# Slots of destination blocks shared in chains of four instead of pairs

## The chip, the cores and the metric

The kernel runs on one NeuronCore of a Trainium2 chip. The metric is the device time of one execution in microseconds (us), the median of three runs. The trace is that of one further execution, taken by the hardware profiler. A core has five engines that run their own instruction streams side by side: TensorE (PE), VectorE (DVE), ScalarE (ACT), GpSimd (POOL) and SyncE (SP).

## The reference

A graph of 3125 nodes with 128 features and 53125 edges, sorted by destination, passes through four graph layers. After each the result is added to x and normalised:

```python
x = _layernorm(x + _L0_gnn_ref(x, deg_isqrt[:, None], src, dst), axis=-1)   # 10 hops of hs[src] summed by dst
x = _layernorm(x + _L1_gnn_ref(x, edge_index, ...), axis=-1)                # two attention (GAT) layers, 4 heads
x = _layernorm(x + _L2_gnn_ref(x, edge_index, edge_type_8, ...), axis=-1)   # h[edge_type, src] * weight summed by dst
x = _layernorm(x + _L3_gnn_ref(x, src, dst, ...), axis=-1)                  # attention of 8 heads, then an MLP
```

Each of L1 (twice), L2 and L3 reads, for every edge, a row of a table at the edge's source, weighs it, and adds it to the edge's destination (`jax.ops.segment_sum(msg, dst, ...)`). The norms and the dense products between them belong to the nodes, not the edges.

## The kernel before

**Blocks, slots, tiles.** The nodes are cut into 25 destination blocks of 128 (`NB`; the last has 53 nodes). A slot, or tile, is 128 edges, one on each partition. Every one of the first 24 blocks has `CAP = 17` slots and the last has 7 (`CAP_TAIL`), 415 in all. Each node's own loop is taken out of the list and treated by itself, so that a block has some 2050 edges and its 17 slots (2176 places) are not quite full.

**Sorting.** `order_edges` packs the edges, counts them by block (PE adds up `in_bin` into `ord_ps`), works out where the 448 slots start in the packed list (`below`, `own_slots` and `column` on PE, then `ord_first` and `ord_start` on DVE) and fetches them with four indirect DMAs of POOL. In a pair of blocks, the second block's slots are shifted back, so that an overhang of the first (what it has above 16 full tiles) and the start of the second lie in the same tile. That tile is then the last slot of the first block and the first slot of the second, and each of the two masks what is not its own. Tests in the same function set `c.uneven`, by which `count_and_choose` later takes a general, edge-by-edge program instead of the blocked one when blocks are too full: here, when a pair has more than 33 tiles of edges.

**The four gather stages.** `layers_by_blocks` runs two attention layers (`Layer`), the relations (`Relations`) and the cross attention (`Cross`). Each is a loop over 25 blocks:

- POOL issues one indirect DMA for each fetched slot, 128 rows of the table by the indices of that slot (L2203 from `gat_table`, L2620 from `rel_table_b`, L2953 from `kv_table_b`), into a ring `t_rows` of two blocks (three in the relations). It waits for `summed` at most before tiles 0 (or 1), 6 and 12 of a block: the slots must have been added up.
- In the attention layers, ACT copies the scores (L2229), PE lays them out (L2281), DVE scans them (L2374 to L2391), ACT takes exponentials (L2240, L2241), DVE weighs the rows (L2403), and PE adds the 17 tiles up in groups of six with one-hot matrices (L2311).
- The shared slot is fetched once. `fetched(b)` leaves out the first tile of an odd block, and for it ACT copies the row tile within the ring (L2233 in the layers, L2968 in the cross attention); the relations read the neighbour's slot directly. For the gathers a stage thus has 415 - 12 = 403 indirect DMAs.

```python
def fetched(b):
    return tiles_of(b)[b % 2:]
def shared(b):
    return b % 2 == 0 and b < NB - 1
```

**Work between.** When a set of blocks is done (`SETS`: five of four blocks, one of two, one of three), its nodes are normalised and turned into rows of the next stage's table, on PE, ACT and DVE within the same loops (L1848 to L1865 in the first layer, L1924 to L2049 in the second). A stage's first gather waits until the whole table is in memory.

Each engine's order is that of the code. Engines meet by semaphores alone.

Of the kernel before, what the change touches and what calls it, by code (L numbers as in the profile page):

```python
# [16 lines left out]
P = 128  # L17
# [3 lines left out]
NB = -(-N // P)  # L21
# [10 lines left out]
BINS = NB + 1  # L32
# [17 lines left out]
PAIRS = (NB - 1) // 2  # L50
PAIR_TILES = 2 * CAP - 1
# [98 lines left out]
def order_edges(c):  # L150
# [20 lines left out]
    with ExitStack() as ctx:  # L171
# [13 lines left out]
        column = c.sb(ctx, "ord_column", [BINS, 3])  # L185
        number, odd = c.sb(ctx, "ord_number", [BINS, 1], i32), c.sb(ctx, "ord_odd", [BINS, 2])
        pair_tot = c.sb(ctx, "ord_pair_tot", [P, PAIRS])
# [13 lines left out]
         prepared, imaged, split, scaled) = (  # L201
# [3 lines left out]
                                        "ends_known", "ends_turned", "prepared", "imaged", "split", "scaled"))  # L205
# [9 lines left out]
        with every_engine(nc) as block:  # L215
# [32 lines left out]
            def _(pool):  # L248
# [13 lines left out]
                p.iota(number[:, :], [[0, 1]], base=0, channel_multiplier=1).then_inc(made, 1)  # L262
# [22 lines left out]
                p.tensor_tensor(own_slots[:, :, :], upto[:, :, :], below[:, :, :], ALU.subtract).then_inc(const, 1)  # L285
                pool.wait_ge(blanked, 16)
# [14 lines left out]
            def _(pe):  # L301
# [28 lines left out]
            def _(dve):  # L330
# [7 lines left out]
                then(v.memset(caps[:, 0:NB - 1], float(CAP)))  # L338
                dve.wait_ge(made, 9)
                v.tensor_scalar(odd[:, 1:2], number[:, :], float(NB - 1), None, ALU.is_lt)  # L340
                then(v.tensor_scalar(number[:, :], number[:, :], 1, None, ALU.bitwise_and))
                then(v.tensor_tensor(odd[:, 0:1], number[:, :], odd[:, 1:2], ALU.mult))
# [77 lines left out]
                v.tensor_scalar(least[:, 0:1], bin_end[0:1, 1:2], float(CAP * P), None, ALU.is_lt)  # L420
                then(v.tensor_tensor(pair_tot[:, :], all_tot[:, 0:NB - 1:2], all_tot[:, 1:NB - 1:2], ALU.add))
                then(v.tensor_reduce(crowded[:, :], pair_tot[:, :], AX, ALU.max))
                then(v.tensor_scalar(crowded[:, :], crowded[:, :], float(PAIR_TILES * P), None, ALU.is_gt))
                then(v.tensor_tensor(least[:, 0:1], least[:, 0:1], crowded[0:1, 0:1], ALU.max))
                then(v.tensor_tensor(c.uneven[:, :], c.uneven[:, :], least[:, 0:1], ALU.max))
# [1165 lines left out]
class Tiles:  # L1591


    def __init__(self, c, ctx, y):
# [21 lines left out]
        self.apart_from = sb("apart_from", [P, PAIRS])  # L1616
# [55 lines left out]
class Enter:  # L1672
# [97 lines left out]
    def merge(self, dve, index, start):  # L1770
# [3 lines left out]
        end = (NB - 1) * CAP  # L1774
        ours, theirs = index[:, CAP - 1:end:2 * CAP], index[:, CAP:end:2 * CAP]
        then(v.tensor_tensor(t.apart_from[:, :], theirs, ours, ALU.subtract))
        then(v.scalar_tensor_tensor(t.apart_from[:, :], t.dst[:, CAP:end:2 * CAP], 0.0, t.apart_from[:, :], ALU.is_ge, ALU.mult))
        v.tensor_tensor(ours, ours, t.apart_from[:, :], ALU.add).then_inc(self.merged, 1)
# [294 lines left out]

# [1915 lines left out]
```

## Time and profile before

| | us |
|---|---|
| median of 3 runs (3307.51 to 3309.09) | 3308.25 |
| the profiled execution | 3306.08 |
| its span, first to last instruction | 3304.3 |
| first layer, first to last gather | 1103.9 to 1613.1 |
| second layer | 1647.8 to 2156.0 |
| relations | 2206.5 to 2712.7 |
| cross attention | 2727.2 to 3234.1 |

The span is what the trace divides. Before the first gather lie the sorting (until 64.5 us), the counting of edges into a dense matrix and ten hops with it; behind the last gather lies the MLP. Busy shares are averages over stages that have little in common, so the stages are read one by one.

### The profile page before, as it was taken

Reading aid. Unit: us, or ns where it says so; the run is one execution under the profiler, and the core shown is the slowest. Engines: PE = TensorE matmul, PEld = TensorE weight load, DVE = VectorE, ACT = ScalarE, POOL = GpSimd, SP = SyncE. Lnnn points to the kernel's source line nnn. Section 1 sums busy time; section 2 is a strip of 40 time slices with the busy share of each in tenths; the row PEclk is TensorE's granted clock in tenths of the full one; section 3 lists DMA queues with packets and bytes.
Section 4 is the critical chain, followed back from the end, with each engine's and each line's share of the span. In section 5 each row is a group of like instructions: output and inputs, shape, how many; then the busy total and the mean of one; then the engine's idle time right before and its main releaser. Section 6 shows DMA issues by size and latency. Waiting matters only on the chain.

```text
span 3304.3 us, 42775 instructions
## 1 busy us (share of the span) xinstructions
PE 2117.3 (64%) x14275; PEld 1831.5 (55%) x14276; DVE 2144.0 (65%) x5718; ACT 1247.9 (38%) x1339; POOL 1814.1 (55%) x1791
## 2 busy tenths in 40 slices
PE   2875999999999456656546666743333344555555
PEld 1554999999999444444435454523333333454444
DVE  7997776776668466666647777754444445555555
ACT  1886667667666323333233333310000002222222
POOL 2333222222222477777477777727777767777771
PEclk7987999999999777777767787766666666666668
DMA  2100000000000644444355555522333224444441
GB/s 64 25 1 1 0 0 0 0 0 0 0 0 0 179 131 141 137 139 137 84 151 144 161 160 160 150 78 72 84 87 95 59 58 132 132 133 133 132 120 39
DMA packets 152192, 274.29 MB, mean 83 GB/s; under 512 B 34026, under 2 KB 96086, under 8 KB 151974
## 3 DMA queue, kind: packets, MB, share of 16 engines
q0 software_dynamic: 72208, 188.45, 21.1%
q1 hardware_dynamic: 43142, 60.09, 5.8%
q10 hardware_dynamic: 36692, 23.93, 2.4%
q8 instruction: 72, 1.18, 0.1%
q14 instruction: 78, 0.64, 0.1%
HBM read 244.71 MB, written 27.85 MB: 82 GB/s over the span
## 4 chain that ended last, share of the span: by engine, by line
POOL 40%; issue 14%; PE 6%; DVE 5%; DMA 2%; ACT 1%; ACTq 0%; POOLq 0%; DVEq 0%
POOL t_rows L2203 19%; POOL t_rows L2620 11%; POOL t_rows L2953 10%; PE t_sum_ps L2311 2%; PE t_sum_ps L2641 1%; PE t_product_ps L1942 1%; DVE t_rows L2403 1%; DMA t_rows<-gat_table,t_src 1%; DMA t_rows<-rel_table_b,t_rel 1%; DMA t_rows<-kv_table_b,t_src 0%; PE t_product_ps L2814 0%; PE t_sum_ps L3013 0%; DVE t_stage L3037 0%; PE t_small_ps L2806 0%; DVE t_stage L3042 0%
## 5 line engine op out<-in xcount | busy, mean ns | idle before, releaser
L2203 POOL DMA_INDIRECT t_rows<-gat_table,t_src x806 | 769.3, 954 | 304.6 <-issue 242.2
L1238 PE MATMUL hop_ps<-parts,wide 128*128 128x256 f32 x5900 | 713.4, 284 | 4.0 <-DVE parts L1334 2.8
L1238 PEld LDWEIGHTS hop_ps<-parts,wide 128*128 128x128 f32 x5900 | 711.1, 192 | 5.7 <-issue 3.3
L1289 ACT CAST wide<-counts 128x3200 fp32r<-128x3200 fp8e4 x177 | 506.3, 2863 | 230.8 <-PE hop_ps L1238 211.2
L2311 PE MATMUL t_sum_ps<-t_rows,t_onehot 128*128 128x264 f32 x1660 | 465.7, 448 | 101.4 <-DVE t_rows L2403 101.4
L1299 POOL CAST wide<-counts 128x3200 fp32r<-128x3200 fp8e4 x59 | 168.7, 2859 | 580.7 <-PE hop_ps L1238 564.6
L2620 POOL DMA_INDIRECT t_rows<-rel_table_b,t_rel x403 | 383.7, 952 | 173.0 <-issue 171.2
L2311 PEld LDWEIGHTS t_sum_ps<-t_rows,t_onehot 128*128 128x128 f32 x1660 | 369.8, 226 | 181.1 <-issue 104.5
L2953 POOL DMA_INDIRECT t_rows<-kv_table_b,t_src x403 | 384.4, 954 | 137.0 <-issue 121.3
L2641 PE MATMUL t_sum_ps<-t_rows,t_onehot 128*128 128x128 f32 x830 | 148.9, 362 | 294.1 <-DMA t_rows<-rel_table_b,t_rel 294.0
L2641 PEld LDWEIGHTS t_sum_ps<-t_rows,t_onehot 128*128 128x128 f32 x830 | 144.6, 275 | 303.8 <-issue 301.8
L2992 PE MATMUL t_small_ps<-t_own,t_turned 128*128 128x128 bf16 x957 | 110.5, 312 | 257.3 <-DVE t_stage L3037 252.2
L2403 DVE TENSOR_TENSOR t_rows<-t_rows,t_sum_ps 128x768 f32<-128x768 f32 (+1 forms) x288 | 251.1, 900 | 15.5 <-ACT t_sum_ps L2241 15.5
L2992 PEld LDWEIGHTS t_small_ps<-t_own,t_turned 128*128 128x128 bf16 x957 | 97.6, 146 | 272.0 <-DVE t_stage L3037 266.7
L2130 DVE TENSOR_TENSOR t_onehot<-t_small_ps,t_dst 128x768 f32<-128x768 f32 (+1 forms) x222 | 194.4, 896 | 0.2
L1076 PE MATMUL cnt_ps<-hot_column,hot_src 128*128 128x320 bf16 x830 | 160.7, 335 | 45.8 <-DVE hot_column L1121 36.2
L2529 ACT COPY t_turned_all<-t_turn_ps 128x512 f32<-128x512 f32 (+2 forms) x7 | 3.8, 539 | 475.1 <-PE t_turn_ps L2509 475.1
L3037 DVE TENSOR_TENSOR t_stage<-t_rows,t_small_ps 128x512 f32<-128x512 f32 x98 | 55.4, 586 | 196.8 <-DMA t_rows<-kv_table_b,t_src 191.5
L2660 DVE TENSOR_TENSOR t_own<-t_own,t_sum_ps 128x128 f32<-128x128 f32 x25 | 7.2, 287 | 264.4 <-PE t_sum_ps L2641 264.4
L2163 ACT ACTIVATE t_apart<-t_dst_wide,t_node 128x2176 f16<-128x2176 f16 (+1 forms) x75 | 153.9, 2052 | 18.1 <-DMA t_dst_wide<-dst_row 17.9
L2167 ACT ACTIVATE t_turned<-t_apart,ones 128x2176 bf16<-128x2176 f16 (+1 forms) x75 | 154.9, 2066 | 2.5
L1076 PEld LDWEIGHTS cnt_ps<-hot_column,hot_src 128*128 128x128 bf16 x830 | 99.9, 147 | 97.5 <-issue 54.9
(443 smaller groups left out, 3291.1 us busy)
## 6 DMA issues: line engine op xcount, KB each, us to landing
t_dst_wide<-dst_row SPq DMA_DIRECT2D x72, 544.0 KB, 4.2
t_rows<-gat_table,t_src POOLq DMA_INDIRECT x806
rel_table_b<-t_stage ACTq DMA_DIRECT2D x25, 512.0 KB, 3.6
t_rows<-rel_table_b SPq DMA_DIRECT2D x18, 512.0 KB, 3.9
t_rows<-rel_table_b,t_rel POOLq DMA_INDIRECT x403, 2.5
t_rows<-kv_table_b,t_src POOLq DMA_INDIRECT x403, 2.8
gat_table<-t_own ACTq DMA_DIRECT2D x10, 520.0 KB, 5.8
kv_table_b<-t_fresh ACTq DMA_DIRECT2D x5, 512.0 KB, 5.1
```

The source lines that it names most:

```text
L1076: last = nc.tensor.matmul(bank[:, h * 512:h * 512 + JH], hot_src[:, g % 2, :, n], hot[:, k % RING, h * JH:(h + 1) * JH], start=(k == ks[0] ...
L1238: last = nc.tensor.matmul(ps[bank][0:columns.shape[-1], 0:2 * D], columns[:, k, :], parts[old][:, k, :], start=(k == 0), stop=(k == NB - 1))
L1289: nc.scalar.copy(wide[b % B][:, :, :], column(b)).then_inc(widened, 1)
L1299: nc.gpsimd.tensor_copy(wide[B - 1][:, :, :], column(b)).then_inc(pool_widened, 1)
L2130: last = v.tensor_tensor(t.onehot[:, hot_at(ks[lo]):hot_at(ks[lo]) + m, :], t.iota.rearrange("p (o d) -> p o d", o=1).to_broadcast([P, m, P]),
L2203: c.nc.gpsimd.indirect_dma_start(t.rows[:, slot(k), 0:FW], None, self.table, bass.IndirectOffsetOnAxis(ap=t.src[:, k:k + 1], axis=0)).then ...
L2311: product = c.nc.tensor.matmul(t.pa[b % 2][:, 0:RW], t.onehot[:, hot_at(k), :], t.rows[:, slot(k), :], start=(n == 0), stop=(n == len(ks) ...
L2403: v.tensor_tensor(h, h, self.weight(b)[:, tiles[0]:tiles[0] + m, :].rearrange("p t (h o) -> p t h o", o=1).to_broadcast([P, m, HEADS, HID] ...
L2620: c.nc.gpsimd.indirect_dma_start(self.rows[:, self.slot(k), :], None, self.table, bass.IndirectOffsetOnAxis(ap=t.rel[:, k:k + 1], axis=0)) ...
L2641: product = c.nc.tensor.matmul(t.pa[b % 2][:, 0:D], t.onehot[:, hot_at(k), :], self.rows[:, self.slot(k - (k not in fetched(b))), :], star ...
L2953: c.nc.gpsimd.indirect_dma_start(t.rows[:, slot(k), 0:2 * D], None, self.table, bass.IndirectOffsetOnAxis(ap=t.src[:, k:k + 1], axis=0)).t ...
L2992: last = c.nc.tensor.matmul(self.looked_ps[j][:, m * P:(m + 1) * P], t.turned[:, b % 2, n * P:(n + 1) * P], query[:, i, :], start=(i == 0) ...
```

## The change

Blocks are chained in fours: blocks 0 to 3, 4 to 7, and so on to 20 to 23. In a chain each block shares a slot with the next, so 18 slots are fetched once and used twice (`SHARED`), where it was 12 (`PAIRS`). The new pairs are blocks 1 and 2, 5 and 6, 9 and 10, 13 and 14, 17 and 18, 21 and 22. A chain fits if no running overhang is above one tile, hence 65 tiles of rows per four blocks.

```diff
-PAIRS = (NB - 1) // 2
-PAIR_TILES = 2 * CAP - 1
+CHAIN = 4
+CHAINED = NB - 1
+SHARED = CHAINED // CHAIN * (CHAIN - 1)
...
 (POOL, order_edges)
+                for n in range(CHAIN - 1):
+                    by_chain = reaches[:, n, :].rearrange("p (q j) -> p q j", j=CHAIN)
+                    p.affine_select(out=by_chain, in_=by_chain, compare_op=ALU.is_ge, fill=0.0,
+                                    base=0, pattern=[[-CHAIN, CHAINED // CHAIN], [0, CHAIN]], channel_multiplier=1).then_inc(const, 1)
... (two more affine_selects of all of reaches)
 (PE, order_edges)
-                pe.wait_ge(const, 8)
+                pe.wait_ge(const, 8 + CHAIN + 1)
                 pe.wait_ge(columns, 3)
+                for n in range(CHAIN - 1):
+                    last = nc.tensor.matmul(ps[3][0:CHAINED, 32 + n:33 + n], reaches[:, n, :], column[:, 3:4], start=True, stop=True)
+                last.then_inc(reached, 1)
+                pe.wait_ge(columns, 4)
 (DVE, order_edges)
-                v.scalar_tensor_tensor(column[:, 2:3], column[:, 0:1], -float(CAP * P), odd[:, 0:1], ALU.add, ALU.mult).then_inc(columns, 1)
+                v.tensor_scalar(column[:, 3:4], column[:, 0:1], -float((CAP - 1) * P), None, ALU.add).then_inc(columns, 1)
                 v.tensor_scalar(spread_tot[:, :], c.ident[0:BINS, 0:BINS], column[:, 0:1], None, ALU.mult).then_inc(spread_known, 1)
+                dve.wait_ge(reached, 1)
+                then(v.tensor_reduce(overhang[:, :], ps[3][0:CHAINED, 32:32 + CHAIN - 1], AX, ALU.max))
+                v.tensor_scalar(column[0:CHAINED, 2:3], overhang[:, :], 0.0, -1.0, ALU.max, ALU.mult).then_inc(columns, 1)
...
+                then(v.tensor_scalar(excess[:, :], all_tot[:, 0:CHAINED], -float((CAP - 1) * P), None, ALU.add))
+                in_chain = excess[:, :].rearrange("p (q j) -> p q j", j=CHAIN)
+                for j in range(1, CHAIN):
+                    then(v.scalar_tensor_tensor(in_chain[:, :, j], in_chain[:, :, j - 1], 0.0, in_chain[:, :, j], ALU.max, ALU.add))
+                then(v.tensor_reduce(crowded[:, :], excess[:, :], AX, ALU.max))
+                then(v.tensor_scalar(crowded[:, :], crowded[:, :], float(P), None, ALU.is_gt))
...
+def begins_shared(b):
+    return b < CHAINED and b % CHAIN > 0
+def copies_before(b):
+    return sum(shared(n) for n in range(b))
 def fetched(b):
-    return tiles_of(b)[b % 2:]
+    return tiles_of(b)[1 if begins_shared(b) else 0:]
 def shared(b):
-    return b % 2 == 0 and b < NB - 1
+    return b < CHAINED and b % CHAIN < CHAIN - 1
...
 (Layer.keep, and alike in the cross attention)
-            if b % 2:
-                act.wait_ge(self.shared, self.shared_before + b // 2 + 1)
+            if begins_shared(b):
+                act.wait_ge(self.shared, self.shared_before + copies_before(b))
```

The unchanged rest of `keep` now runs for blocks 1, 5, 9 and so on too: before its copy ACT waits for the first group of sums of the block before (`groups_through((b - 1) * CAP)`).

On ACT, at block 1 of the first layer (the names: `t_es` scores, `t_rows` the ring, `t_logit` the weights' logarithms), the rows before are

```order
L2229 COPY t_es<-t_rows 128x68
L2240 ACTIVATE t_rows<-t_logit 128x17x4
L2241 ACTIVATE t_sum_ps<-t_logit 128x68
L2213 ACTIVATE t_own_w<-t_own_l,t_own_twice 128x4
L2219 ACTIVATE t_own<-t_own,t_own_w 128x64 x4
```

and now

```order
L2257 COPY t_es<-t_rows 128x68
L2261 COPY t_rows<-t_rows 128x260
L2268 ACTIVATE t_rows<-t_logit 128x17x4
L2269 ACTIVATE t_sum_ps<-t_logit 128x68
L2241 ACTIVATE t_own_w<-t_own_l,t_own_twice 128x4
L2247 ACTIVATE t_own<-t_own,t_own_w 128x64 x4
```

One copy of a row tile has come between the copy of the scores and the exponentials; it stands in this place in six more blocks of each attention layer, and so does its like in the cross attention.

On DVE, in `order_edges` behind the count of the edges, the rows before are

```order
L375 TENSOR_REDUCE ord_column<-ord_ps 26x1
L377 TENSOR_SCALAR ord_column<-ord_column 26x1
L378 SCALAR_TENSOR_TENSOR ord_column<-ord_column,ord_odd 26x1
L379 TENSOR_SCALAR ord_spread_tot<-ident,ord_column 26x26
L381 TENSOR_TENSOR ord_first<-ord_slot_at,ord_ps 112x4
L382 TENSOR_SCALAR ord_start<-ord_first 112x4
```

and now

```order
L389 TENSOR_REDUCE ord_column<-ord_ps 26x1
L391 TENSOR_SCALAR ord_column<-ord_column 26x1
L392 TENSOR_SCALAR ord_column<-ord_column 26x1
L393 TENSOR_SCALAR ord_spread_tot<-ident,ord_column 26x26
L395 TENSOR_REDUCE ord_overhang<-ord_ps 24x1
L396 TENSOR_SCALAR ord_column<-ord_overhang 24x1
L398 TENSOR_TENSOR ord_first<-ord_slot_at,ord_ps 112x4
L399 TENSOR_SCALAR ord_start<-ord_first 112x4
```

Two operations have come in ahead of `ord_first`, and between them and the columns PE now has three products with `ord_reaches`.

On POOL the four stages' gathers read before (both attention layers share a row)

```order
IOTA t_node 128x1
DMA t_rows<-gat_table,t_src 128x260 x806
DMA t_rows<-rel_table_b,t_rel 128x128 x403
DMA t_rows<-kv_table_b,t_src 128x256 x403
```

and now 794, 397 and 397 of the same DMAs: each stage has lost one in blocks 2, 6, 10, 14, 18 and 22.

## Rows read from the trace of the kernel before

**Rows 1.** The page: busy time, shares of the chain that ended last, costliest group.

```profile
PE 2117.3 (64%) x14275; PEld 1831.5 (55%) x14276; DVE 2144.0 (65%) x5718; ACT 1247.9 (38%) x1339; POOL 1814.1 (55%) x1791
...
POOL 40%; issue 14%; PE 6%; DVE 5%; DMA 2%; ACT 1%; ACTq 0%; POOLq 0%; DVEq 0%
...
L2203 POOL DMA_INDIRECT t_rows<-gat_table,t_src x806 | 769.3, 954 | 304.6 <-issue 242.2
```

**Rows 2.** Stages: length; PE, PEld, DVE, ACT, POOL busy; clock; DMA share, GB/s.

```profile
1104.00:1613.00 509.00, 295.10 (x1423) 230.44 (x1423) 335.90 (x822) 161.35 (x275) 386.55 (x403) 0.72 0.50 140
1648.00:2156.00 508.00, 325.04 (x1563) 239.53 (x1563) 347.10 (x888) 180.92 (x313) 382.39 (x403) 0.77 0.55 154
2206.00:2713.00 507.00, 183.56 (x892) 160.91 (x892) 229.24 (x797) 17.31 (x34) 383.65 (x403) 0.64 0.29 77
2727.00:3234.00 507.00, 250.00 (x2101) 235.34 (x2102) 291.27 (x571) 128.54 (x126) 384.33 (x403) 0.68 0.44 130
```

**Rows 3.** POOL's waits, whole span: total, times, longest; then line L2203.

```profile
POOL t_rows L2203 <- issue: 242.2, 795, 0.3
...
POOL t_rows L2203 <- PE t_sum_ps L2311: 5.9, 9, 3.5
...
L2203 POOL DMA_INDIRECT t_rows<-gat_table,t_src x806: 941/946/3751, 1103.9 to 2155.1; - x162
```

**Rows 4.** Timeline of POOL, second layer, first gather of block 23.

```profile
2127.32 1.18 POOL L2203 DMA_INDIRECT t_rows<-gat_table,t_src  x1 [3.46 <-PE t_sum_ps L2311]
```

**Rows 5.** Chain that ended last, second layer, from block 20's landing: start, us.

```profile
2081.54 3.48 DMA t_rows<-gat_table,t_src
...
2121.22 3.16 PE t_product_ps L1942 x6
2124.38 5.79 PE t_sum_ps L2311 x26
```

**Rows 6.** First layer, block 22 lands: a row of the chain, two of the timeline.

```profile
1583.39 2.74 DMA t_rows<-gat_table,t_src
...
1575.56 10.09 PE L2311 MATMUL t_sum_ps<-t_rows,t_onehot 128*128 128x264 f32 x34 [2.59 <-DVE t_rows L2403]
...
1586.46 0.68 PE L2281 MATMUL t_small_ps<-ident,t_es 128*68 128x64 f32 x6 [0.82 <-ACT t_es L2229]
```

**Rows 7.** The same chain where relations and cross attention end.

```profile
2711.71 3.27 DMA t_rows<-rel_table_b,t_rel
...
3224.39 2.71 DMA t_rows<-kv_table_b,t_src
```

**Rows 8.** First layer: block 17's first six sums; POOL starts block 19.

```profile
1493.02 5.49 PE L2311 MATMUL t_sum_ps<-t_rows,t_onehot 128*128 128x264 f32 x12 [2.64 <-DVE t_rows L2403]
...
1501.71 0.95 POOL L2203 DMA_INDIRECT t_rows<-gat_table,t_src  x1 [0.30 <-issue]
```

**Rows 9.** The copy within the ring (min/median/max ns); ACT's waits before exponentials.

```profile
L2233 ACT COPY t_rows<-t_rows x24: 402/402/403, 1127.9 to 2130.9; 128x260 f32<-128x260 f32 x24
...
ACT t_rows L2240 <- DVE t_logit L2390: 238.2, 50, 10.3
```

**Rows 10.** Timeline of the sorting, from POOL's wait to the last test.

```profile
36.61 1.14 POOL L291 DMA_INDIRECT edges_in_order<-ord_rows,ord_chunk_to  x1 [17.57 <-DVEq L369]
...
44.24 0.14 DVE L378 SCALAR_TENSOR_TENSOR ord_column<-ord_column,ord_odd 26x1 f32<-26x1 f32 x1
...
44.52 0.32 PE L314 MATMUL ord_ps<-ord_column,ord_below 26*112 26x1 f32 x2 [1.07 <-DVE ord_column L378]
...
46.09 0.92 PE L319 MATMUL ord_ps<-ord_column,ord_upto 26*112 26x1 f32 x8
...
46.26 0.16 DVE L381 TENSOR_TENSOR ord_first<-ord_slot_at,ord_ps 112x4 f32<-112x4 f32 x1 [1.73 <-PE ord_ps L315]
...
56.52 0.14 DVE L420 TENSOR_SCALAR ord_least<-ord_bin_end 1x1 f32<-1x1 f32 x1
...
57.53 0.39 DVE L430 CAST ord_code_i<-x 112x256 int32<-112x256 f32 x1
```

More of the change, by code:

```diff
@@ L184, in order_edges @@
         crowded = c.sb(ctx, "ord_crowded", [P, 1])
-        column = c.sb(ctx, "ord_column", [BINS, 3])
-        number, odd = c.sb(ctx, "ord_number", [BINS, 1], i32), c.sb(ctx, "ord_odd", [BINS, 2])
-        pair_tot = c.sb(ctx, "ord_pair_tot", [P, PAIRS])
+        column = c.sb(ctx, "ord_column", [BINS, 4])
+        reaches = c.sb(ctx, "ord_reaches", [BINS, CHAIN - 1, CHAINED])
+        overhang = c.sb(ctx, "ord_overhang", [CHAINED, 1])
+        excess = c.sb(ctx, "ord_excess", [P, CHAINED])
         below, upto, own_slots = (c.sb(ctx, f"ord_{n}", [BINS, SLOT_PARTS, CK]) for n in ("below", "upto", "own_slots"))
@@ L261, in _ @@
                 p.memset(pick[:, :, :], 0.0).then_inc(made, 1)
-                p.iota(number[:, :], [[0, 1]], base=0, channel_multiplier=1).then_inc(made, 1)
+                p.memset(reaches[:, :, :], 1.0).then_inc(made, 1)
                 pool.wait_ge(made, 9)
@@ L285, in _ @@
                 p.tensor_tensor(own_slots[:, :, :], upto[:, :, :], below[:, :, :], ALU.subtract).then_inc(const, 1)
+                for n in range(CHAIN - 1):
+                    by_chain = reaches[:, n, :].rearrange("p (q j) -> p q j", j=CHAIN)
+                    p.affine_select(out=by_chain, in_=by_chain, compare_op=ALU.is_ge, fill=0.0,
+                                    base=0, pattern=[[-CHAIN, CHAINED // CHAIN], [0, CHAIN]], channel_multiplier=1).then_inc(const, 1)
+                pool.wait_ge(const, 8 + CHAIN - 1)
+                p.affine_select(out=reaches[:, :, :], in_=reaches[:, :, :], compare_op=ALU.is_ge, fill=0.0,
+                                base=-1, pattern=[[0, CHAIN - 1], [1, CHAINED]], channel_multiplier=-1).then_inc(const, 1)
+                pool.wait_ge(const, 8 + CHAIN)
+                p.affine_select(out=reaches[:, :, :], in_=reaches[:, :, :], compare_op=ALU.is_ge, fill=0.0,
+                                base=1, pattern=[[1, CHAIN - 1], [-1, CHAINED]], channel_multiplier=1).then_inc(const, 1)
                 pool.wait_ge(blanked, 16)
@@ L338, in _ @@
                 then(v.memset(caps[:, 0:NB - 1], float(CAP)))
+                then(v.memset(column[:, :], 0.0))
                 dve.wait_ge(made, 9)
-                v.tensor_scalar(odd[:, 1:2], number[:, :], float(NB - 1), None, ALU.is_lt)
-                then(v.tensor_scalar(number[:, :], number[:, :], 1, None, ALU.bitwise_and))
-                then(v.tensor_tensor(odd[:, 0:1], number[:, :], odd[:, 1:2], ALU.mult))
                 dve.wait_ge(dst_loaded, 48)
@@ L419, in _ @@
                 then(v.scalar_tensor_tensor(c.bin_start[:, :], bin_end[:, :], -1.0, all_tot[:, :], ALU.add, ALU.subtract))
[L420 to L425, printed above, removed]
+                then(v.tensor_scalar(excess[:, :], all_tot[:, 0:CHAINED], -float((CAP - 1) * P), None, ALU.add))
[4 more added lines that the diff above has]
+                then(v.tensor_scalar(crowded[:, :], crowded[:, :], float(P), None, ALU.is_gt))
+                then(v.tensor_tensor(c.uneven[:, :], c.uneven[:, :], crowded[0:1, 0:1], ALU.max))
                 src, rel, dst, made_of = (field(c.by_slot, f) for f in (SRC, REL, DST, CODE))
@@ L1773, in merge @@
         then = chained(dve, self.merged, start)
[L1774 to L1778, printed above, removed]
+        by_chain = [tile[:, 0:CHAINED * CAP].rearrange("p (q j s) -> p q j s", j=CHAIN, s=CAP) for tile in (index, t.dst)]
+        ours, theirs = by_chain[0][:, :, 0:CHAIN - 1, CAP - 1], by_chain[0][:, :, 1:CHAIN, 0]
+        then(v.tensor_tensor(t.apart_from[:, :, :], theirs, ours, ALU.subtract))
+        then(v.scalar_tensor_tensor(t.apart_from[:, :, :], by_chain[1][:, :, 1:CHAIN, 0], 0.0, t.apart_from[:, :, :], ALU.is_ge, ALU.mult))
+        v.tensor_tensor(ours, ours, t.apart_from[:, :, :], ALU.add).then_inc(self.merged, 1)
     def dve(self, dve):
@@ L2927, in __init__ @@
         self.tabled, self.split = before.tabled, before.split
-        self.shared, self.shared_before = t.shared, 2 * PAIRS
+        self.shared, self.shared_before = t.shared, 2 * SHARED
         super().__init__(c, "cross")
@@ L2970, in act @@
             if shared(b):
[L2971 removed]
+                act.wait_ge(self.shared, self.shared_before + copies_before(b + 1))
             score = t.score[:, b % 2, 0:n, :]
@@ L3046, in scores @@
             dve.wait_ge(self.gathered[b % RING_BLOCKS], arrived(b))
-            if b % 2:
-                dve.wait_ge(self.shared, self.shared_before + b // 2 + 1)
+            if begins_shared(b):
+                dve.wait_ge(self.shared, self.shared_before + copies_before(b))
             if b >= 2:
```

11 lines of the change are left out of this document (5 added, 6 removed).

## The prediction

> **What bounds the kernel now.** I read the page first, then the four gather stages by windows, then POOL's waits, then the chain where each stage ends.
>
> The page shows no engine busy for more than 65% of the span, but on the chain that ended last POOL has 40% and "issue" 14% [rows 1]. "Issue" there is mostly the short pause ahead of each gather: 242.2 us in 795 pauses are 0.305 us each [rows 3]. The gather itself has a median of 946 ns [rows 3]. So POOL begins a gather every 1.25 us. 403 gathers make 504 us, and the windows of the four stages are 507 to 509 us long [rows 2]. Each stage is thus POOL issuing one gather after the other, with nothing between. The other engines are busy there for 347 us at most (DVE, second layer) [rows 2]. What would break this is POOL waiting for a free slot of the ring. In both layers that is 5.9 us in nine waits [rows 3], and one wait of 3.46 us, at block 23 of the second layer [rows 4], is more than the usual 0.3 pause; the other eight are that pause.
>
> **What goes.** Each stage loses six gathers, in blocks 2, 6, 10, 14, 18 and 22. At 1.25 us each this is 7.5 us per stage on the engine that bounds it. Whether all of it reaches the stage's end depends on what the end hangs on.
>
> - First layer: the chain to the end starts from the landing of block 22, whose last gather began at 1583.39 [rows 6]. All six dropped gathers lie before it, so it lands 7.5 us earlier. But the distance to the block before shrinks by 1.25 us, and PE is adding up block 21 until 1585.65 (1575.56 + 10.09), while it started on block 22 at 1586.46 [rows 6]. Only 0.81 of the 1.25 us can be taken there; 0.44 is lost. Gain 7.1.
> - Second layer: the sums of block 21 start at 2124.38, at the end of a chain of products and norms that began with the landing of block 20 (gather of 2081.54) [rows 5]. POOL waits for them at block 23 [rows 4]. Block 20's landing has five of the six dropped gathers before it and comes 6.25 us earlier; the chain behind it is as long as before. The sixth gather, in block 22, only lets POOL come to its wait 1.25 us sooner. The wait becomes 4.7 us, and the rest of the stage hangs on it. Gain 6.25.
> - Relations: the end hangs on the landing of the very last gather [rows 7]. The ring has three blocks and ACT copies nothing. Gain 7.5.
> - Cross attention: the end hangs on the landing of block 23 [rows 7], behind all six. Gain 7.5.
>
> Together 28.3 us.
>
> **What the price of one gather is taken from.** The row says that the next gather starts 1.25 us after the last, whatever it moves: the relations move 77 GB/s and the second layer 154, at the same length of stage [rows 2]. The sum by the row is 24 x 1.25 = 30 us before the losses above. The Trainium skill (DMA: Bandwidth & Descriptors, section "Anatomy of one DMA") speaks against so much: it calls descriptor generation small and puts a DMA's time at about 2.0 us fixed, mostly completion, plus bytes over 436 GB/s. The fixed part overlaps with the next gather, and an estimate from that page for what 133 KB add is 0.3 us, so the sum by it would be at most some 7 us.
>
> **What comes in.**
>
> - In the layers, ACT copies a row tile in six more blocks, 0.402 us each [rows 9]. It stands between the copy of the scores, which starts PE's work, and the exponentials. ACT has been idle ahead of the exponentials for 238.2 us in 50 blocks, 4.8 each [rows 9], so the copy is covered; without that cover it would cost 0.4 us on the chain of a block, and only where that chain ends a stage would it be seen, block 21 of the second layer at most. In the cross attention six more copies of the same size stand ahead of ACT's wait for the scores, which come behind the same landing. The copy also waits for the first sums of the block before. That must have happened for POOL to have filled the slots of the block behind it, and block 17 of the first layer shows the distance: its first six sums end at 1498.5 (1493.02 + 5.49), 3.2 us before POOL starts block 19 at 1501.71 [rows 8]. I take nothing.
> - The slack of blocks 1, 5, 9 and so on shrinks, for POOL needs 20.0 instead of 21.25 us for the block behind. Block 17 of the first layer has the least, 3.2 us [rows 8]; 1.25 and a copy of 0.4 leave 1.5. Nothing waits. If I am wrong by 2 us there, five such blocks cost 0.5 us each.
> - In the sorting, PE has three more products between two DVE steps, and the `ord_start` that POOL waits for comes later. Four products like them take 0.92 us [rows 10], so three 0.69. DVE's reduction reads PSUM like L381, 0.16; the operation behind it 0.14 like L378; PE starts 0.14 behind its input (44.38 to 44.52) [rows 10], and two handovers between engines or instructions take some 0.06. That is 1.2 us, all on the chain, since DVE itself waited for PE here (1.73) [rows 10]. Further on, six small test operations (56.52 to 57.53, 0.17 each) become seven, four of them wider: 1.3 instead of 1.0. Together 1.5 us. From below, the products alone are 0.7; from above, two full waits like the 1.07 of PE [rows 10] more make 3. The new operations of POOL (a memset, five selects) lie in its wait of 17.57 us before it writes the packed edges [rows 10] and are hidden there; uncovered they would be some 3 us, at about 0.5 each.
>
> **The sum.** 28.3 - 1.5 = 26.8 us. The profiled execution took 3306.08, so 3279.3; the median lies 2.2 us above the profiled time, so 3281.4 us.
>
> **The rivals.**
>
> - Part of it is swallowed again by the ring. Ten blocks of the two layers follow a finished set of blocks, and PE and DVE then carry more work; if each made POOL wait 1 us, 10 us would go: 3291. Against it: the only real wait is block 23's [rows 4], and busy engines have a third of the stage free [rows 2].
> - Gathers are bound by the bytes they move, not by POOL's time. Then each dropped one frees only the DMA engines' share, 0.50, 0.55, 0.29 and 0.44 [rows 2] of 7.5 us: 13.4 us, less the sorting 12: 3296. Against it: one pace at all four shares. This is the direction of the skill's page.
> - Slower than before: the new wait and copy on ACT hold up the exponentials of blocks 1, 5, 9, 13, 17 and 21 so long that the ring runs empty. Their slack after the change is about 2 to 3 us in the first layer and 6 in the second by my reading of block 17 [rows 8] and its likes, and block 21 of the second has none [rows 4]. A delay of 7 us costs some 22, 7 and 5 us in the first layer, the second and the cross attention: more than 33, which is 26.8 and 0.2% of the span. It decides from about 7 us on, where 0.4 is the copy's length [rows 9]: only if the first sums of a block came 12 us later than they do. Time 3316.
> - The chains don't fit and the general program is taken. I counted the edges of the reference's inputs: the largest running overhang is 125 of the 128 that the test allows, in the fifth chain; the margin is 3 edges. If the counts were others, each stage would fetch 448 slots instead of 403, 225 us more by the gathers alone: above 3500.
>
> **How the numbers follow.** My forecast 0.86; swallowed in part 0.06; bytes 0.03; slower by ACT 0.02; general program 0.01; 0.02 for what I don't see, near no change. The forecast's own range is 3276 to 3286: 5 us below if the second layer gives all six gathers (1.25), the sorting costs 0.7, and a rare long gather (maximum 3751 ns [rows 3]) stays away; 5 above for one or two more of these or 3 us in the sorting. The range to hold 8 in 10 reaches to the rival of the ring, 3275 to 3289. A difference within 0.2% of the time (6.6 us) is about what a measurement can't tell from none. Faster by more than that: 0.95; within it: 0.02; slower: 0.03.
>
> **What the profile after would show.** 794, 397 and 397 gathers at an unchanged pace; stages shorter by 7 to 7.5 us, the second layer by 6.3 with a wait of 4.7 at block 23; the copy 18 times in each layer at 0.40 us with the exponentials no later behind a block's landing; the first row behind the sorting 1.5 us later. The prediction is wrong if POOL's waits for PE's sums grow at other blocks, if the pace changes, or if the general program runs.

## The result, and the profile after

The changed kernel takes 3281.08 us (median of 3 runs, 3280.29 to 3281.26) where the kernel before takes 3308.25: a ratio of 0.9921 with a 95% interval of 0.9908 to 0.9934. The forecast was 3281.4. The profiled execution took 3281.08 us as well, with a span of 3279.3 where it was 3304.3.

The page of the changed kernel, with the rows that answer to [rows 1]:

```profile
PE 2113.7 (64%) x14281; PEld 1829.1 (56%) x14282; DVE 2144.2 (65%) x5719; ACT 1254.9 (38%) x1357; POOL 1794.8 (55%) x1772
...
POOL 38%; issue 13%; DVE 7%; PE 7%; DMA 2%; ACT 1%; ACTq 0%; POOLq 0%; DVEq 0%
...
L2231 POOL DMA_INDIRECT t_rows<-gat_table,t_src x794 | 759.5, 957 | 302.3 <-issue 239.1
```

The four stages by windows, cut from the first to the last gather as in [rows 2] (length; PE, PEld, DVE, ACT, POOL busy; clock; DMA share, GB/s):

```profile
1107.00:1609.00 502.00, 296.26 (x1423) 231.01 (x1423) 336.69 (x824) 163.22 (x281) 381.05 (x397) 0.73 0.50 141
1644.00:2146.00 502.00, 322.73 (x1563) 239.19 (x1563) 347.03 (x887) 183.24 (x319) 377.61 (x397) 0.77 0.55 154
2195.00:2696.00 501.00, 183.07 (x892) 160.82 (x892) 229.28 (x798) 17.31 (x34) 379.01 (x397) 0.66 0.28 77
2710.00:3210.00 500.00, 250.50 (x2108) 235.65 (x2109) 292.14 (x572) 130.30 (x129) 378.26 (x397) 0.68 0.44 130
```

Six gathers are gone from each, the length fell by 6 to 7 us, and the rest hardly moved: DMA share and bandwidth within 0.01 and 1 GB/s, the granted clock within 0.02, the busy times of PE, DVE and ACT within 2.4 us. Only POOL's busy time fell with the length, by 4.6 to 6.1 us.

POOL's waits after, as in [rows 3] (total, times, longest):

```profile
POOL t_rows L2231 <- issue: 239.1, 785, 0.3
...
POOL t_rows L2231 <- PE t_sum_ps L2339: 5.6, 7, 3.8
```

The pause is still 239.1 / 785 = 0.305 us, and no new wait for PE has come. The 3.8 is the wait at block 23 of the second layer, which was 3.46 us in [rows 4]:

```profile
2117.05 1.18 POOL L2231 DMA_INDIRECT t_rows<-gat_table,t_src  x1 [3.80 <-PE t_sum_ps L2339]
```

The chain that ended last, second layer, from the landing of block 20 to the relations' table (compare [rows 5]; start, us, what):

```profile
2072.11 2.72 DMA t_rows<-gat_table,t_src
...
2111.36 2.75 PE t_product_ps L1960 x6
2114.11 7.57 PE t_sum_ps L2339 x34
...
2190.89 3.53 DMA rel_table_b<-t_stage
```

No gather stands between the first and the last of these rows.

Where the 25.0 us of span went. A stage is counted here from its first gather to the first gather of the next, the cross attention to the end of the span:

| | before | after | difference | forecast |
|---|---|---|---|---|
| up to the first gather | 1103.9 | 1106.5 | +2.6 | +1.5 |
| first layer | 543.9 | 537.2 | -6.8 | -7.1 |
| second layer | 558.7 | 551.8 | -6.9 | -6.25 |
| relations | 520.7 | 514.2 | -6.5 | -7.5 |
| cross attention to the end | 577.1 | 569.7 | -7.4 | -7.5 |

In the sorting the timeline of DVE and PE reads, as in [rows 10]:

```profile
46.83 0.16 DVE L398 TENSOR_TENSOR ord_first<-ord_slot_at,ord_ps 112x4 f32<-112x4 f32 x1 [1.82 <-PE ord_ps L331]
...
47.72 1.63 PE L335 MATMUL ord_ps<-ord_column,ord_below 26*112 26x1 f32 x8
...
49.38 0.16 DVE L403 SCALAR_TENSOR_TENSOR ord_front<-ord_first,ord_ps 112x4 f32<-112x4 f32 x1 [1.08 <-PE ord_ps L335]
...
58.05 0.18 DVE L437 TENSOR_SCALAR ord_excess<-ord_all_tot 128x24 f32<-128x24 f32 x1
...
59.46 0.39 DVE L448 CAST ord_code_i<-x 112x256 int32<-112x256 f32 x1
```

The first row behind the sorting's tests, the CAST, stands at 59.46 where it stood at 57.53: 1.93 later. `ord_first` is 0.57 later; the tests of the chains take 1.41 (58.05 to 59.46) instead of 1.01; the remaining 1.0 comes at L403, which now waits 1.08 us for PE's products of L335 (before: 0.17 us for L319, the same products). What made them slow is TensorE's granted clock. It fell from 1.0 to 0.5 (2.4 to 1.2 GHz) at 47.60 us before and at 47.15 us after, while the products begin later than before. The windows of their second half (start and end; length, PE busy, clock, DMA share, GB/s) are those of the kernel before, of the changed one, and of a kernel with the same sorting in which the clock fell only at 49.53 (that of "Is the wait at block 23 lost time?" with chains of four):

```profile
46.88:47.87 0.99, 0.99 (x10) 0.86 0.00 0
...
47.72:49.35 1.63, 1.63 (x9) 0.50 0.00 0
...
48.63:49.55 0.92, 0.92 (x10) 0.99 0.00 0
```

One of these products starts 0.10 us behind the last at the clock of 1.0 and 0.19 us behind it at 0.5. From the reduction of the counts to the CAST it is 13.97 us before, 16.06 in the changed kernel and 15.02 where the clock held: about 1.1 us are the sorting's new work, and about 1.0 is the lower clock that it runs into here.

### The profile page after: what moved, and what is told of

The parts are those of the page before. It is cut to its first block, busy times and chain, and to the rows that moved or that the text cites. A ratio compares the mean times of both kernels' runs of the same rounds, so it can differ in the third digit from the quotient of the medians.

```text
span 3279.3 us, 42810 instructions
## 1 busy us (share of the span) xinstructions
PE 2113.7 (64%) x14281; PEld 1829.1 (56%) x14282; DVE 2144.2 (65%) x5719; ACT 1254.9 (38%) x1357; POOL 1794.8 (55%) x1772
## 4 chain that ended last, share of the span: by engine, by line
POOL 38%; issue 13%; DVE 7%; PE 7%; DMA 2%; ACT 1%; ACTq 0%; POOLq 0%; DVEq 0%
POOL t_rows L2231 17%; POOL t_rows L2648 10%; POOL t_rows L2981 10%; PE t_sum_ps L2339 2%; DVE t_rows L2431 1%; PE t_sum_ps L2669 1%; DVE t_onehot L2158 1%; DMA t_rows<-rel_table_b,t_rel 1%; DMA t_rows<-gat_table,t_src 1%; PE t_small_ps L2309 0%; DMA t_rows<-kv_table_b,t_src 0%; PE t_product_ps L1960 0%; PE t_small_ps L2834 0%; PE t_product_ps L2842 0%; DVE t_stage L3065 0%
## 5 line engine op out<-in xcount | busy, mean ns | idle before, releaser
L2231 POOL DMA_INDIRECT t_rows<-gat_table,t_src x794 | 759.5, 957 | 302.3 <-issue 239.1
L2648 POOL DMA_INDIRECT t_rows<-rel_table_b,t_rel x397 | 379.0, 955 | 170.4 <-issue 168.5
L2981 POOL DMA_INDIRECT t_rows<-kv_table_b,t_src x397 | 378.6, 954 | 135.1 <-issue 119.1
```

The lines of the kernel that those rows point to most:

```text
L2231: c.nc.gpsimd.indirect_dma_start(t.rows[:, slot(k), 0:FW], None, self.table, bass.IndirectOffsetOnAxis(ap=t.src[:, k:k + 1], axis=0)).then ...
L2648: c.nc.gpsimd.indirect_dma_start(self.rows[:, self.slot(k), :], None, self.table, bass.IndirectOffsetOnAxis(ap=t.rel[:, k:k + 1], axis=0)) ...
L2981: c.nc.gpsimd.indirect_dma_start(t.rows[:, slot(k), 0:2 * D], None, self.table, bass.IndirectOffsetOnAxis(ap=t.src[:, k:k + 1], axis=0)).t ...
```

## The experiments

Ratios are to the kernel before, run on the same chip. Chips differ a little (3305.9 to 3311.3 us for the kernel before), so kernels are compared by ratio, and by their traces where less than 0.2% matters.

### The sorting alone, and no sharing at all

The first kernel sorts for chains of four but shares slots in pairs only:

```diff
-SHARED = CHAINED // CHAIN * (CHAIN - 1)
+SHARED = CHAINED // 2
 def begins_shared(b):
-    return b < CHAINED and b % CHAIN > 0
+    return b < CHAINED and b % 2 > 0
 def shared(b):
-    return b < CHAINED and b % CHAIN < CHAIN - 1
+    return b < CHAINED and b % 2 < 1
```

> The sorting of the change (chains of four) with the sharing of before: the gather stages fetch 403 slots and copy 12 tiles, as pairs do. Isolates what the sorting costs. My theory: about 2 us more than before, 3310.2 (the trace after the change shows the first operation behind the tests 1.9 us later), and gather stages as before. Rival: the sorting is hidden, 3308.3. Rival: it costs 5 or more, and the gathers bring more than I said, 3313 and above.

Measured: 3308.74 us, ratio 1.0008 (0.9999 to 1.0017). That is +2.6 us with an interval of -0.3 to +5.6; the sign is not settled by the times. Its trace shows nearly the same delay: the CAST of L448 stands at 59.23, with a wait of 1.15 us before L403 and the clock down to 0.5 from 46.82. So the price of the sorting is about 2 us, and the rest of the change is worth some 29 by the ratios (1.0008 to 0.9921) and 27.5 by the two spans (3306.8 to 3279.3).

The second is the kernel before with every slot fetched anew, 415 gathers per stage instead of 403:

```diff
 def fetched(b):
-    return tiles_of(b)[b % 2:]
+    return tiles_of(b)
 def shared(b):
-    return b % 2 == 0 and b < NB - 1
+    return False
... (the waits for `shared` of odd blocks go with it)
```

> The kernel before with no sharing at all: all 415 slots fetched in each of the four stages, no copies within the ring. It takes the theory of the gather's price the other way, by 12 gathers per stage. Mine (POOL issues one each 1.25 us): relations and cross attention 15 us longer, the first layer 13.75 (11 of the 12 lie before the landing of block 22), the second 12.5 (10 before that of block 20): 56 us, 3364.5. By bytes moved (the stages' DMA shares of 15 us each): 27 us, 3335. By the page's variable part (0.3 us each): 14 us, 3323.

Measured: 3364.3 us, ratio 1.0173 (1.0158 to 1.0189), +57 us for 48 gathers more, 1.19 us each (1.09 to 1.30 by the interval). Its trace gives 62.0 in the span (3366.3), 1.29 each; the layers took 16.5 and 13.8 us more, where 13.75 and 12.5 were expected, and the relations and the cross attention 14.5 and 15.9. So the price of a gather holds in the other direction too, to about a tenth.

### Half the bytes

Each gather of the cross attention leaves out half of its row, so that the last layer computes on other numbers; the instructions and their order are the same.

> The change, with each gather of the cross attention moving half the bytes (it leaves out half of each row and reads the table as twice as many rows, so the last layer computes on other numbers). Mine: POOL's time per gather doesn't depend on them, the pace stays 1.25 us, 3281. By bytes: half of the stage's DMA share of 0.44 goes, 397 x 1.25 x 0.22 = 109 us: 3172. By the page's variable part (0.15 us each of 397): 3221.

```diff
-c.nc.gpsimd.indirect_dma_start(t.rows[:, slot(k), 0:2 * D], None, self.table,
+c.nc.gpsimd.indirect_dma_start(t.rows[:, slot(k), 0:D], None, self.table.rearrange("n (h f) -> (n h) f", h=2),
```

Measured: 3281.99 us, ratio 0.9927 (0.9912 to 0.9943), against 0.9921 for the change. The window of its cross attention:

```profile
2713.00:3211.00 498.00, 249.99 (x2106) 235.14 (x2106) 291.43 (x571) 130.10 (x129) 376.92 (x397) 0.68 0.28 79
```

and the group of its gathers on its page (count, busy us, mean ns, idle time ahead):

```profile
L2981 POOL DMA_INDIRECT t_rows<-kv_table_b,t_src x397 | 377.2, 950 | 135.0 <-issue 119.5
```

The bandwidth fell from 130 to 79 GB/s and the DMA share from 0.44 to 0.28, while a gather's mean went from 954 ns (378.6 us in 397) to 950 and the window from 500 to 498. Here a gather of 128 rows cost POOL its 0.95 us and the pause with rows of 1024 and of 512 bytes alike. This rejects the rival that the gathers are bound by bytes. The Trainium skill (DMA: Bandwidth & Descriptors, section "Anatomy of one DMA") puts the size into the time of one DMA and calls descriptor generation small; the prediction's estimate from it for the whole change was at most 7 us, and the runs show 27.

### Chains of six

```diff
-CHAIN = 4
+CHAIN = 6
```

> Chains of six instead of four: 20 shared slots, 395 gathers per stage. The largest running overhang of these edges in sixes is 91 of 128, so they fit. Mine: 2 gathers less in each stage, both before the landings that the ends hang on, 10 us, less some 0.5 in the sorting (two more products, two more test operations): 3271.6. Rival: the ring's slack is used up in the layers, POOL waits there, half of the gain goes: 3276. If the general program ran: above 3500.

Measured: 3271.98 us (3271.06 to 3274.7), ratio 0.99 (0.9885 to 0.9915), the lowest of all kernels here. Two gathers fewer in each stage and a chain of two more products in the sorting. Its windows:

```profile
1108.00:1607.00 499.00, 293.57 (x1423) 229.66 (x1423) 337.39 (x825) 163.88 (x283) 378.70 (x395) 0.73 0.50 141
1641.00:2141.00 500.00, 322.32 (x1564) 239.40 (x1565) 347.37 (x889) 183.39 (x321) 375.22 (x395) 0.76 0.54 154
2190.00:2687.00 497.00, 176.35 (x888) 153.67 (x889) 228.53 (x795) 17.32 (x34) 376.91 (x395) 0.64 0.28 77
2701.00:3198.00 497.00, 249.41 (x2101) 234.74 (x2102) 291.52 (x571) 131.73 (x134) 376.68 (x395) 0.68 0.44 130
```

The span is 9.8 us below that of chains of four (3269.5), and eight gathers at 1.25 are 10. The ratio's distance, 0.0021, is 7 us, and the two intervals (0.9885 to 0.9915 and 0.9908 to 0.9934) overlap a little; the kernel with half the bytes, chains of four on the same chip as this one, took 3281.99 us, 10.0 more. The four-block chain is thus no optimum. Six is the longest chain that these inputs allow: the largest running overhang is 91 edges with chains of six (125 with four), counted from the edges of the reference's inputs, and would be 135, above the 128 of a tile, with eight, twelve or twenty-four.

### How far ACT's copy is from hurting

The next three kernels repeat the copy of the shared row tile in blocks 1, 5, 9, 13, 17 and 21 of both attention layers, which the change gave a copy for the first time. The edit, for 24 more copies:

```diff
             if shared(b):
+                done = self.shared_before + self.copies_before(b)
+                for n in range(24 if b % CHAIN == 1 else 0):
+                    done += 1
+                    c.nc.scalar.copy(t.rows[:, slot((b + 1) * CAP), 0:FW], t.rows[:, slot((b + 1) * CAP - 1), 0:FW]).then_inc(self.shared, 1)
+                    act.wait_ge(self.shared, done)
                 c.nc.scalar.copy(t.rows[:, slot((b + 1) * CAP), 0:FW], t.rows[:, slot((b + 1) * CAP - 1), 0:FW]).then_inc(self.shared, 1)
... (`shared_before` and `copies_before` count the further copies)
```

With 8 more:

> The change, with the new copy of ACT in blocks 1, 5, 9, 13, 17 and 21 of both layers done nine times, one after the other, instead of once: 8 x 0.42 = 3.4 us more ahead of the exponentials. Mine: ACT is idle for 4 us and more there, so it is covered: 3281 to 3282. Rival (the copy lies on the blocks' chain, and the ring has no slack left): 12 x 3.4, above 3300.

Measured: 3283.16 us, ratio 0.9914 (0.9901 to 0.9928), span 3279.4 against 3279.3. Nothing is lost: the 96 further copies (39.1 us of ACT in all) lie in its wait for the scores' logarithms, which fell from 237.7 to 198.3 us.

With 24 more:

> The same with 24 more copies, 10.2 us. Mine: some 4 us are covered, so the exponentials of six blocks in each layer come 6 to 6.5 us later. The ring's slack after the change is 3.0 to 3.4 us in the first layer's blocks 5, 9, 13, 17 and 21 and 5.0 to 6.3 in the second's 5 to 17, so POOL waits some 3.3 us five times and 0.3 to 1.5 four times: 20 to 25 us, 3303. If copies never mattered: 3281. If all of it lay on the chain: 12 x 10, 3400.

Measured: 3318.64 us, ratio 1.0025 (1.0016 to 1.0035), span 3314.3. The loss is 35 us in the span, well over what I had put. ACT's timeline in block 5 of the first layer, in the changed kernel

```profile
1239.16 0.25 ACT L2257 COPY t_es<-t_rows 128x68 f32<-128x68 f32 x1 [0.52 <-ACT t_own L1883]
1239.31 0.40 ACT L2261 COPY t_rows<-t_rows 128x260 f32<-128x260 f32 x1
1243.91 0.26 ACT L2268 ACTIVATE t_rows<-t_logit 128x68 f32<-128x68 f32 x1 [4.20 <-DVE t_logit L2418]
```

and with 24 more copies, with POOL's row at block 7 (start, us, engine, what, wait):

```profile
1238.22 0.25 ACT L2260 COPY t_es<-t_rows 128x68 f32<-128x68 f32 x1 [0.51 <-ACT t_own L1883]
1238.37 10.53 ACT L2267 COPY t_rows<-t_rows 128x260 f32<-128x260 f32 x24
...
1249.43 0.26 ACT L2276 ACTIVATE t_rows<-t_logit 128x68 f32<-128x68 f32 x1
...
1256.45 0.95 POOL L2234 DMA_INDIRECT t_rows<-gat_table,t_src  x1 [4.10 <-PE t_sum_ps L2347]
```

A copy that waits for the one before it comes every 0.439 us (10.53 / 24), not every 0.402. The exponentials come 11.21 us behind the copy of the scores instead of 4.75, a delay of 6.46. In the changed kernel block 5's first six sums end 3.3 us before POOL would wait for them (block 7), so some 3.2 us of wait are left, and the row shows 3.8 above the usual pause. The first layer has five such waits. In the second layer the copying blocks have 6.3 to 5.0 us of slack, which would leave little. But POOL waits there one block later, and longer than I had put:

```profile
1830.42 0.95 POOL L2234 DMA_INDIRECT t_rows<-gat_table,t_src  x1 [3.03 <-PE t_sum_ps L2347]
...
2001.15 1.18 POOL L2234 DMA_INDIRECT t_rows<-gat_table,t_src  x1 [4.19 <-PE t_sum_ps L2347]
```

These are the first gathers of blocks 8 and 16, which wait for blocks 6 and 14. PE's timeline of the changed kernel shows why, at block 18, which stands like them:

```profile
2044.82 2.34 PE L1960 MATMUL t_product_ps<-t_w_rel,t_turned_all 128*128 128x512 f32 x6 [0.45 <-ACT t_stage L2058]
2047.00 6.17 PE L2339 MATMUL t_sum_ps<-t_rows,t_onehot 128*128 128x264 f32 x27
```

The products of the finished set stand in front of the sums of blocks 6, 10, 14 and 18 there. Block 18's first six sums (12 of the 27 matmuls) end at about 2049.8, and POOL starts block 20 at 2052.11: 2.3 us of slack, where the copying block before it has 5.0. What block 17 is late is handed on to block 18, and the smaller slack decides. Beyond the usual pause and the wait at block 23 of the second layer, POOL's waits for PE come to some 32 us, nearly all of the 35.

To test that reading on numbers not used for it, 20 more copies:

> The change, with the copy within the ring done 21 times instead of once in blocks 1, 5, 9, 13, 17 and 21 of both attention layers; the result is the same. It repeats the kernel with 25 copies at a smaller dose, to see which block's slack sets the loss. There ACT's 24 extra copies took 10.53 us (0.439 each) and the exponentials of block 5 came 11.21 us behind the copy of the scores instead of 4.75, a delay of 6.46 us. With 20 extra copies the delay is 6.46 - 4 x 0.439 = 4.70 us. Theory: in the first layer the slack that counts is that of the blocks that copy (3.3, 3.3, 3.1, 3.0, 3.4 us for blocks 5, 9, 13, 17, 21), so five waits of 1.4 to 1.7, and by the 0.4 that each had more with 25 copies some 9 us; in the second layer it is the slack of the blocks behind them, which inherit the delay (4.0, 3.1, 2.4, 2.3 us for blocks 6, 10, 14, 18), so four waits of 0.7, 1.6, 2.3 and 2.4, 7 us; block 21 adds 0.6. Together 16 to 17 us over the change, 3297 to 3300 us, and POOL waits at the first gathers of blocks 8, 12, 16 and 20 of the second layer. Rival: in the second layer too it is the slack of the copying blocks (6.3, 5.6, 5.1, 5.0), more than the delay; then no wait there and 9 to 10 us in all, 3290 to 3293 us.

Measured: 3298.41 us, ratio 0.9976 (0.9967 to 0.9985), span 3293.6. POOL's waits for PE in the layers are 22.5 us in 17, and the rows of the first gathers of blocks 8 and 16 of the second layer show

```profile
1818.20 0.94 POOL L2234 DMA_INDIRECT t_rows<-gat_table,t_src  x1 [1.21 <-PE t_sum_ps L2347]
...
1982.64 1.18 POOL L2234 DMA_INDIRECT t_rows<-gat_table,t_src  x1 [0.92 <-PE t_sum_ps L2347]
```

The waits stand at the blocks that the theory named (8, 12, 16, 20), where the rival had none. The sizes are off in the second layer: 3.8 us above the pause in the four waits, where I had 7. The first layer has 9.7 (I had 9). The time, 3298.41, is in the theory's range, but the loss against the change is 18 us by the ratios and 14.3 by the spans. The theory had 16 to 17 and the rival 9 to 10. So the place of the waits is shown, and their size in the second layer is half of what the slack gave.

### Is the end of the second layer bound by gathers?

The prediction gave up the sixth dropped gather there: behind block 20's landing everything hangs on PE and DVE. Three gathers more, into a buffer that nobody reads, are put behind the first gather of block 18 (ahead of block 20) or of block 22 (behind it), and ACT waits for them with the block's own rows:

```diff
+for n in range(3 if self.number == 1 and k == fetched(18)[0] else 0):
+    c.nc.gpsimd.indirect_dma_start(t.aside[:, n, :], None, self.table,
+                                   bass.IndirectOffsetOnAxis(ap=t.src[:, k + n:k + n + 1], axis=0)).then_inc(self.gathered[0], 16)
... (the buffer `t.aside`; ACT's wait for `gathered` goes up by 16 * 3 from that block on)
```

> The change, with three more gathers into a tile aside, on POOL, behind the first gather of block 18 in the second layer only. They lie before the landing of block 20. Mine: 3.75 us longer, 3284.8, the second layer 3.75 longer, the wait at block 23 as before (3.8). Rival (the wait at block 23 takes them): no change.

> The same three gathers behind the first gather of block 22. Mine: they are swallowed by POOL's wait at block 23, which falls from 3.8 to 0.3 us; the stage is 0.25 us longer: 3281.3. Rival (the stage hangs on POOL's work all through): 3284.8.

Measured: 3289.66 us and 3282.88, ratios 0.9933 (0.992 to 0.9947) and 0.9912 (0.9898 to 0.9925). The intervals just overlap, so the traces decide. At block 18 the three are there at POOL's pace,

```profile
2013.07 0.95 POOL L2235 DMA_INDIRECT t_aside<-gat_table,t_src  x1 [0.30 <-issue]
...
2120.63 1.18 POOL L2232 DMA_INDIRECT t_rows<-gat_table,t_src  x1 [4.05 <-PE t_sum_ps L2343]
```

the wait at block 23 stays (4.05), and from the first to the end of the last gather the layer takes 505.5 us, where it took 502.1. At block 22

```profile
2096.88 0.95 POOL L2235 DMA_INDIRECT t_aside<-gat_table,t_src  x1 [0.30 <-issue]
...
2119.47 0.95 POOL L2232 DMA_INDIRECT t_rows<-gat_table,t_src  x1 [0.30 <-issue]
```

no wait is left at block 23 and the layer takes 502.5: 3.75 us of gathers cost 3.5 in the one place and 0.4 in the other. Behind block 20 there were some 3.5 us in which gathers cost next to nothing.

### Is the wait at block 23 lost time?

The table rows of the nodes' blocks 16 and 17 are worked out in front of block 22's sums instead of block 21's, with chains of four and with chains of six:

```diff
+LATE[22] = LATE.pop(21) + LATE.get(22, [])
```

> The change, with the table rows of nodes' blocks 16 and 17 worked out on PE and ACT in front of block 22's sums in the second layer instead of block 21's. Block 21's first six sums, for which POOL waits 3.8 us at block 23, then come some 5 us earlier, and the wait goes. Theory: the wait lies on no path: from the landing of block 20 on, the chain of the second layer runs through PE, DVE and the norms without any gather, and the moved products stay on it, only later. Then the time stays at 3281 us, within 1.5 either way, with no wait of POOL left at block 23 and the relations' first gather where it was. Rival: the wait is lost time, and its 3.5 us reach the end of the stage: 3277 to 3278 us.

> Chains of six blocks together with the later products of blocks 16 and 17. Theory: the products' place is worth nothing, and the time is that of chains of six alone, 3272 us within 1.5. Rival: the wait of 4.0 us at block 23 was lost time, and 3.7 us of it come back: 3268 us.

Measured: 3283.84 us, ratio 0.9928 (0.9914 to 0.9941), and 3276.35 us, ratio 0.991 (0.9897 to 0.9924). Neither is faster than the same kernel without the edit (0.9921 and 0.99). The rival's 3.5 and 3.7 us less would be ratios of 0.991 and 0.9889, just below the two intervals. But the edit doesn't take the wait away. The wait at block 23 is gone, and POOL has one of 4.0 us (4.2 with chains of six) at block 24 instead. So what a kernel without a wait would take, these two don't show; that the wait at block 23 holds up nothing is shown by the three gathers of the section before, which filled it at a cost of 0.4 us. My own theory, no change, doesn't hold in the traces either: the second layer, to the relations' first gather, takes 555.6 us instead of 551.8 with chains of four, and 553.3 instead of 548.5 with chains of six. The chain there, with chains of four (start, us, what):

```profile
2121.44 3.67 PE t_product_ps L1960 x4
2125.13 0.59 ACT t_stage L2058
2125.77 2.00 PE t_product_ps L1960 x4
2127.79 0.59 ACT t_stage L2058
2128.43 2.00 PE t_product_ps L1960 x4
2130.45 0.59 ACT t_stage L2058
2131.08 2.34 PE t_product_ps L1960 x6
2133.43 7.57 PE t_sum_ps L2340 x34
...
2193.68 3.52 DMA rel_table_b<-t_stage
```

Both lots of products now stand in one queue ahead of block 22's sums, 12 us with ACT's copies in between (2121.44 to 2133.43). From the last gather of block 20 to the relations' first it is 126.9 us instead of 123.3, and 127.8 instead of 123.3 with chains of six. Not all of these 3.6 and 4.5 us need be the products' place, for the granted clock behind the layer's last gather was 0.76 with the edit and 0.80 without it. Kernels without the edit in which it was 0.76 or 0.77 have 125.0 to 125.2 us there, 1.8 to 2.9 less. The times, with intervals that overlap, say 2 to 3, on the side of the original.

## Why the prediction was right, and where its terms were off

- **The number.** Forecast 3281.4 us, measured 3281.08. So close a hit is luck: the interval of the ratio is 4.3 us wide to each side. The forecast took the median to lie 2.2 us above the profiled execution, and here the two were the same. The sum itself had 26.8 us, and the profiled execution gained 25.0.
- **The bound and the pace.** Right. POOL issuing one gather every 1.25 us sets all four stages. Fewer gathers (chains of four, of six), more (no sharing), and lighter ones (half the bytes) all follow it; the price per gather was 1.19 us by the times of 48, and 27.6 us for 24 in the trace of the change, 1.15 each, where the prediction had 28.3 left of 24 x 1.25.
- **First layer, 7.1.** Measured 6.8. Block 22's last gather stands 7.4 us earlier counted from the first (1583.39 - 1103.92 against 1578.62 - 1106.51), and the rest of the stage is 0.6 longer, where I had 0.44 for PE still adding up block 21. Whether there is such a loss is not settled: from that gather to the second layer's first it is 64.46 us before and 65.04 after, but 64.45 to 65.18 in the other kernels whose block 22 fetches 16 slots too (the two with 20 and 24 more copies left out). That the loss would be PE's was argued from its rows, not tried.
- **Second layer, 6.25.** Measured 6.9, and right in kind: the three gathers set aside behind block 20 were free, those ahead of it were not. The numbers hide two errors that cancel. Block 20's last gather came 5.25 us earlier, not 6.25 (the stage's gathers have a mean of 952 ns, where it was 949), and the chain behind was 1.65 shorter, where I had it as long as before. Of this, 0.85 lies ahead of block 23's first gather: from block 20's last gather it is 44.94 us instead of 45.79, and the landing itself took 2.72 instead of 3.48 [rows 5]. That is why the wait at block 23 was 3.8, where I had 4.7. The other 0.8 lies behind the layer's last gather. From its end to the relations' first gather the kernels that leave this part alone have 50.5 to 51.4 us where the granted clock was 0.76 or 0.77 there, and 48.2 to 49.7 where it was 0.80 or 0.81. The kernel before is of the first kind (0.77) and the changed one of the second (0.80), with PE busy for 32 of the 51 us. So these 0.8 us go with the clock and not with the gathers; no run tried it by itself.
- **Relations, 7.5.** Measured 6.5. The missing 1.0 is in the gathers themselves: POOL's busy time fell from 383.7 [rows 2] to 379.0, where six at 0.946 are 5.7. Their mean went from 952 ns (383.7 in 403) to 955 (379.0 in 397). Why, no run shows; the kernel with the new sorting and the old sharing has 953.
- **Cross attention, 7.5.** Measured 7.4.
- **The sorting, 1.5.** Measured 1.9 at the CAST, and the term was put together wrongly. The products, reduction and hand-overs ahead of `ord_first` were less than I had: 0.7 from column to column, not 1.2. The three products take 0.28, not 0.69, for they are 24 columns wide and the ones that I had read are 112. The tests were 0.1 more. What the term left out is the granted clock, which fell to 0.5 while L335 ran: its second half took 1.63 us where it took 0.99, and DVE waited for it. In the kernels with this sorting in which the clock fell at 48.96 us or later, it took 0.92 to 1.03 us. The other 0.7 us up to the first gather lie within the scatter: kernels with this sorting have their first gather at 1105.8 to 1108.7.
- **ACT's copies, nothing.** Right: they take 0.403 us each, and nine of them in a row in the six new blocks of each layer cost nothing either. But the cover that I gave for the second layer, 6 us of slack, was read from the copying blocks; the next block's, 2.3 to 4.0, is the smaller, and POOL's waits came there. The rival "ACT holds up the exponentials" did come true in kind with 25 copies, slower than before at a delay of 6.5 us (I had put the point at 7), but the change, with one copy of 0.4 us, is far from there.
- **Ring and general program.** The waits for PE fell (5.9 to 5.6 us) and 397 gathers ran, not 448.

## What to carry to other kernels

Where one engine issues transfers back to back, count instructions on that engine, not bytes, and then ask of each one dropped whether it lies ahead of the last landing on which the stage's chain hangs; behind it, it is worth nothing. Read the slack of a ring not only at the block that becomes late but also at the tightest block behind it, since lateness is handed on. A visible wait on the bounding engine needn't be lost time: before moving work to remove it, look whether the chain that ends last runs through it at all (filling the wait with work that nobody needs tries it), and what else stands where the work would go. Before a difference of a microsecond between two traces is put down to the edit, compare the granted clock of that stretch.

## What the runs showed of the hardware

- In the changed kernel a gather of 128 rows took POOL 957, 955 and 954 ns in the mean and 0.30 us of pause with rows of 1040, 512 and 1024 bytes, and 950 with half of the 1024 in the same place.
- One gather in the first layer and one in the cross attention takes 3.1 to 4.0 us in every kernel. In the changed kernel it is the last of block 2, the 49th gather of the stage (the 49th to the 55th in the others):

```profile
1166.99 3.99 POOL L2231 DMA_INDIRECT t_rows<-gat_table,t_src  x1 [0.30 <-issue]
```

  and in the cross attention always the ninth. The second layer and the relations have none. The cause was not looked for.
- A copy of 128x260 on ACT took 0.402 us by itself and 0.439 in a row where each waits for the one before.
- In the sorting, small products of PE (26 rows, 112 columns) started 0.10 us apart at a granted clock of 1.0 and 0.19 us apart at 0.5. When it fell differed from kernel to kernel, from 46.8 to 49.5 us, and moved DVE's next operation by up to 1 us.
